# A mixture-of-experts stage in tiles of 128 rows instead of 256, with the biases prepared by GpSimd

## The chip, the cores and the metric

The kernel runs on one core of a Trainium2 chip. The metric is the device time of one execution in microseconds (us). The engines are TensorE (PE in the profile; PEld is its weight load), VectorE (DVE), ScalarE (ACT), GpSimd (POOL) and SyncE (SP, which here only issues DMAs). Each has its own sequencer, which carries out register arithmetic, waits and branches; the profile marks those with a q (PEldq is TensorE's sequencer).

## What is computed

The reference takes x (8 batches of 512 tokens, 256 wide), adds a gated cross attention, and then a gated mixture of experts, both behind a layer norm:

```python
x = x + tanh(g_xattn) * xattn(layernorm(x), ctx, Wq, Wkv, Wc)
x = x + tanh(g_ffn) * ffn(layernorm(x), gate_w, w1, b1, w2, b2)

def ffn(x, gate_w, w1, b1, w2, b2):          # 8 experts, 2 per token
    top_v, top_i = top_k(x @ gate_w, 2)
    comb = zeros(N, E).at[token, top_i].add(softmax(top_v))
    for e in range(8):
        h = gelu(x @ w1[e] + b1[e])          # 256 -> 1024
        out = out + comb[:, e] * (h @ w2[e] + b2[e])
```

In the attention each token takes the one row of the context with the highest score, and then attends with 16 heads over the rows so taken. The change lies in the mixture of experts.

## The kernel before

**Two stages.** `flow` is the first stage, up to about 520 us: attention, layer norm and gating, batch by batch, in a pipeline whose order is written out by hand in steps. Meanwhile the experts' weights are loaded, split into a bf16 high and a bf16 low part, and kept in SBUF (`w_split`). For each of its two experts, every token's normalised row is scattered by GpSimd into that expert's queue in HBM (L611). A row in a queue has 260 numbers: 256 values, the two weights of the token (already times tanh of the gate), its first expert, and its token number. At the end `tile_tables` (L144 to L172, on VectorE) works out for each tile of rows which expert it belongs to (`expert_of`) and where in `queue` it starts (`row_of`), and SyncE writes a tile of padding rows behind the end of each queue (`pad_queues`, L175). `general_select` and `general_attend` are a slow path, skipped at run time (the branch of `in_general`, L2200), which isn't taken with these inputs.

**The experts' stage** (`experts`, in the functions below) runs over `N_TILES` tiles of `TILE` rows. All rows of a tile belong to one expert; a queue's last tile is padded, and tiles left over are read from a block of padding rows. 8 x 512 tokens with 2 experts give 8192 rows, so with `TILE` 256 there are (8192 + 8 x 255)//256 = 39 tiles, 9984 rows. Each engine has a program of its own, a body per tile, and `over_tiles` (L2216) runs it: some tiles written out, the rest in a loop on the engine (L2220) with two bodies, so that buffers alternate. They meet by semaphores only:

- SyncE reads the tile's number of row into a register and loads the rows (`load`, L2243), two tiles ahead, once `x_turned` and `tail_taken` say that the buffer is free. Before the first loads it issues those of all b1 and b2 (L2239, L2240).
- TensorE's body i (L2408) is `turn(i+1)`, `layer1(i)`, `layer2(i-1)`. `turn` transposes the rows into `ps_x`. `layer1` reads the tile's expert into a register (`load_expert`, L2229) and does 48 matmuls: for each of 8 blocks f of the 1024 hidden values, 2 halves kt of the input, and three products (high weight with high and low x, low weight with high x). The weights are stationary, the tile's rows move. They go to four banks `ps_h` of two blocks each; each bank waits until the gelu of the tile before has read it. `layer2` has the hidden values stationary, 128 tokens at a time, and the weights w2, 256 columns, moving: 2 x 24 matmuls, after all of `h_lo`. In both, the weights' address depends on the register with the expert (L2390, L2404).
- ScalarE's body i: `x_hi` of tile i+1 (a cast to bf16, L2288), then eight gelu with b1 added (L2299), two for each bank.
- VectorE's body i: `prepare(i+1)` (the rows' last four columns into `tails`, the expert's b1 into `bias`, the weight of each row, and `x_lo`), then `h_lo` in four pieces (L2356: the hidden values less their bf16 high part), then `finish(i-1)`: second layer plus b2 (L2342), times the row's weight (L2345).
- GpSimd's body i (L2264): the token numbers as integers (L2269, L2271), then two indirect DMAs of 128 rows (L2273) that add y to the output in HBM. A tile's adds wait for those of the tile before.

```python
def layer2(i, s):
    e = load_expert(pe, i)
    pe.wait_ge(h_lo_ready, PAIRS * (i + 1))
```

Of the kernel before, what the change touches and what calls it, by code (L numbers as in the profile page):

```python
# [22 lines left out]
TILE = 2 * P  # L23
# [120 lines left out]
def tile_tables(v, chain, k, scratch):  # L144

    table = N_TILES * E
    mine, past = (scratch[:, c * table:(c + 1) * table].rearrange("p (i e) -> p i e", e=E) for c in range(2))
    full = scratch[:, 2 * table:2 * table + E * (QUEUE // TILE)].rearrange("p (e n) -> p e n", e=E)
    first_row = scratch[:, 2 * table + E * (QUEUE // TILE):][:, 0:N_TILES]
# [12 lines left out]
    chain.step(v.tensor_reduce(k.valid[:], mine, AX.X, ALU.add))  # L162
# [5 lines left out]
    chain.then(v.tensor_scalar(k.left[:], k.tile_row[:], -float(DUMMY), None, ALU.add))  # L168
    chain.then(v.tensor_tensor(k.valid[:], k.valid[:], k.left[:], ALU.mult))
    chain.then(v.scalar_tensor_tensor(out=k.valid[:], in0=k.valid[:], scalar=float(DUMMY), in1=first_row, op0=ALU.add,  # L170
                                      op1=ALU.add))
    chain.then(v.tensor_copy(k.row_of[:], k.valid[:]))  # L172


def pad_queues(sp, k, padded, before):  # L175

    for at in [sp.value_load(k.pad_at[0:1, n:n + 1], min_val=0, max_val=DUMMY) for n in range(E)]:
        sp.dma_start(k.queue[bass.ds(at, TILE)].rearrange("(s p) c -> p s c", p=P), k.padding[:, None, :].to_broadcast([P, 2, ROW])).then_inc(padded, 16)
    sp.wait_ge(padded, 16 * (before + E))


def program(nc, x, ctx_t, g, wq_t, wkv_t, wc_t, gate_w, w1, b1_t, w2, b2, out):
# [11 lines left out]
    with ExitStack() as whole:  # L194
# [30 lines left out]
        k.valid, k.left = sb(whole, "valid", [P, N_TILES]), sb(whole, "left", [P, N_TILES])  # L225
# [7 lines left out]
        flow(nc, k, sem, sb, ps)  # L233

        general = Programs(), Programs()
        general_select(nc, k, sem, sb, ps, general[0])
        general_attend(nc, k, sem, sb, ps, general[1])
# [3 lines left out]
def flow(nc, k, sem, sb, ps):  # L241
# [6 lines left out]
    with ExitStack() as own:  # L248
# [180 lines left out]
        def _(sp):  # L429
# [65 lines left out]
            sp.dma_start(k.queue[DUMMY:DUMMY + TILE].rearrange("(s p) c -> p s c", p=P), k.padding[:, None, :].to_broadcast([P, 2, ROW])).then_inc(k.padded, 16)  # L495
# [277 lines left out]
        def _(dve):  # L773
# [232 lines left out]
            tile_tables(v, chain, k, x_in[:].rearrange("p t d -> p (t d)"))  # L1006
# [1160 lines left out]
def experts(nc, k, sem, sb, ps, general):  # L2167
    with ExitStack() as own:
# [3 lines left out]
        xg = [sb(own, f"xg{s}", [P, 2, ROW]) for s in range(2)]  # L2172
        tails = sb(own, "tails", [P, N_TILES, 2, 4])
        weight = sb(own, "weight", [P, N_TILES, 2])
        part_a, part_b = sb(own, "part_a", [P, 2]), sb(own, "part_b", [P, 2])
        bias = [sb(own, f"bias{s}", [P, FC]) for s in range(2)]
        x_hi = [sb(own, f"x_hi{s}", [P, KT, TILE], BF16) for s in range(2)]
# [4 lines left out]
        y = [sb(own, f"y{s}", [P, 2, D]) for s in range(2)]  # L2182
        token_f, token_at = sb(own, "token_f", [P, 2]), sb(own, "token_at", [P, 2], I32)

        ps_x = ps(own, "ps_x", [P, KT, TILE])
        ps_h = [ps(own, f"ps_h{n}", [P, 2, TILE]) for n in range(FC // 2)]
        ps_y = [ps(own, f"ps_y{s}", [P, 2, D]) for s in range(2)]
# [3 lines left out]
        tail_taken, x_hi_ready, x_lo_ready = sem("tail_taken"), sem("x_hi_ready"), sem("x_lo_ready")  # L2191
        h_ready, gelu_done, h_lo_ready = sem("h_ready"), sem("gelu_done"), sem("h_lo_ready")
        y_summed, y_biased, y_weighted, added = sem("y_summed"), sem("y_biased"), sem("y_weighted"), sem("added")
        dve_steps, pool_steps = k.dve_steps, k.pool_steps
        PAIRS = FC // 2

        select_met, attend_met, pads_placed, tables_met = (sem("select_met"), sem("attend_met"), sem("pads_placed"),
                                                           sem("tables_met"))

        def in_general(engine, select_all, attend_all, finish=None):  # L2200
            flag = engine.value_load(k.wide[0:1, 0:1], min_val=0, max_val=1)  # L2201
            with engine.If(flag > 0):
                select_all(engine)
# [12 lines left out]
        def over_tiles(engine, body):  # L2216

            body(0, 0, 0, True, True)
            body(1, 0, 1, True, True)
            with engine.Fori(1, (N_TILES - 3) // 2) as j:  # L2220
                body(2 * j, j, 0, True, True)
                body(2 * j + 1, j, 1, True, True)
# [3 lines left out]
        def first(i, n=1):  # L2226
            return isinstance(i, int) and i < n

# [4 lines left out]
        def _(sp):  # L2233
# [4 lines left out]
            in_general(sp, general[0].sp, general[1].sp, pad)  # L2238
            sp.dma_start(b1_sb[:], k.b1_t).then_inc(bias_loaded, 16)  # L2239
# [3 lines left out]
            def load(i, s):  # L2243
                row = sp.value_load(k.row_of[0:1, bass.ds(i, 1)], min_val=0, max_val=DUMMY)  # L2244
                sp.dma_start(xg[s][:], k.queue[bass.ds(row, TILE)].rearrange("(s p) c -> p s c", p=P)).then_inc(row_loaded[s], 16)

            def body(i, half, s, more, two_more):
                if two_more:

                    sp.wait_ge(x_turned, i + 1)  # L2250
                    sp.wait_ge(tail_taken, i + 1)
                    load(i + 2, s)

            load(0, 0)
            load(1, 1)
# [3 lines left out]
        def _(pool):  # L2259
            in_general(pool, general[0].pool, general[1].pool)  # L2260
# [3 lines left out]
            def body(i, half, s, more, two_more):  # L2264
                if not first(i):

                    pool.wait_ge(added, 32 * i)
                pool.wait_ge(y_weighted, i + 1)
                chain.then(g.tensor_tensor(token_f[:], tails[:, bass.ds(i, 1), :, 3].rearrange("p a s -> p (a s)"),  # L2269
                                           k.ones_f[:, 0:2], ALU.mult))  # L2270
                chain.then(g.tensor_copy(token_at[:], token_f[:]))  # L2271
                for t in range(2):
                    pool.indirect_dma_start(k.out_rows, bass.IndirectOffsetOnAxis(ap=token_at[:, t:t + 1], axis=0),  # L2273
                                            y[s][:, t, :], None, bounds_check=B * L - 1, oob_is_err=False,
                                            compute_op=ALU.add).then_inc(added, 16)
                chain.restart()

            over_tiles(pool, body)
            pool.wait_ge(added, 32 * N_TILES)

        @block.scalar
        def _(act):
# [7 lines left out]
            def body(i, half, s, more, two_more):  # L2290
                if more:
                    split_x(i + 1, 1 - s)
                if not first(i, 2):
                    act.wait_ge(y_summed, i - 1)
                for n in range(PAIRS):
                    act.wait_ge(h_ready, PAIRS * i + n + 1)
                    for c in range(2):
                        f = 2 * n + c
                        last = a.activation(hidden[s][:, f, :], ps_h[n][:, c, :], ACT.Gelu, bias=bias[s][:, f:f + 1])  # L2299
# [6 lines left out]
        def _(dve):  # L2306
# [3 lines left out]
            def tables():  # L2310
                pad_places(v, chain, k, pads_placed)
                tile_tables(v, chain, k, hidden[0][:].rearrange("p f t -> p (f t)"))
# [3 lines left out]
            dve.wait_ge(bias_loaded, 32)  # L2316

            def prepare(i, half, s):


                e = load_expert(dve, i)
                dve.wait_ge(row_loaded[s], 16 * (half + 1))
                tail = tails[:, bass.ds(i, 1)].rearrange("p a s c -> p (a s) c")
                v.tensor_copy(tail, xg[s][:, :, D:ROW]).then_inc(tail_taken, 1)
                v.tensor_copy(bias[s][:], b1_sb[:, bass.ds(e, 1), :].rearrange("p a f -> p (a f)"))
                dve.wait_ge(tail_taken, i + 1)
                this = k.tile_expert[:, bass.ds(i, 1)]
                chain.step(v.scalar_tensor_tensor(out=part_a[:], in0=tail[:, :, 2], scalar=this, in1=tail[:, :, 0],
                                                  op0=ALU.is_equal, op1=ALU.mult))
                chain.then(v.scalar_tensor_tensor(out=part_b[:], in0=tail[:, :, 2], scalar=this, in1=tail[:, :, 1],  # L2330
                                                  op0=ALU.not_equal, op1=ALU.mult))
                chain.step(v.tensor_tensor(weight[:, bass.ds(i, 1), :].rearrange("p a s -> p (a s)"), part_a[:], part_b[:], ALU.add))
# [3 lines left out]
            def finish(i, s):  # L2336
                dve.wait_ge(y_summed, i + 1)
                if not first(i, 2):
                    dve.wait_ge(added, 32 * (i - 1))
                e = load_expert(dve, i)  # L2340
                b2_own = b2_all[:, bass.ds(e, 1), :].to_broadcast([P, 2, D])
                v.tensor_tensor(y[s][:], ps_y[s][:], b2_own, ALU.add).then_inc(y_biased, 1)  # L2342
                dve.wait_ge(y_biased, i + 1)
                for t in range(2):
                    last = v.tensor_scalar(y[s][:, t, :], y[s][:, t, :],  # L2345
                                           weight[:, bass.ds(i, 1), t:t + 1].rearrange("p a s -> p (a s)"), None, ALU.mult)
# [102 lines left out]
```

## Time and profile before

| | us |
|---|---|
| Median of 3 runs | 994.2 |
| Lowest and highest | 994.14, 994.46 |
| Span of the profiled execution, first to last instruction | 992.7 |
| What lies around the span, as the median less the span | 1.5 |
| PE busy | 832.3 (84%) |
| VectorE busy | 517.9 (52%) |
| GpSimd busy | 438.1 (44%) |
| ScalarE busy | 376.7 (38%) |

The profile comes from one execution. Its own time is known as its span; the runs' times are those of whole executions. Spans and windows count from its first instruction. A matmul's record lasts until its result is written, so records of one stream overlap, and the distance between starts is what a matmul costs there. Register arithmetic, loads of a register (TENSOR_LOAD) and waits don't count as busy; they appear in the view of a single line, with the engine's name and a q.

### The profile page before, as it was taken

Reading aid. Unit: us, or ns where it says so; the run is one execution under the profiler, and the core shown is the slowest. Engines: PE = TensorE matmul, PEld = TensorE weight load, DVE = VectorE, ACT = ScalarE, POOL = GpSimd, SP = SyncE. Lnnn points to the kernel's source line nnn. Section 1 sums busy time; section 2 is a strip of 40 time slices with the busy share of each in tenths; the row PEclk is TensorE's granted clock in tenths of the full one; section 3 lists DMA queues with packets and bytes.
Section 4 is the critical chain, followed back from the end, with each engine's and each line's share of the span. In section 5 each row is a group of like instructions: output and inputs, shape, how many; then the busy total and the mean of one; then the engine's idle time right before and its main releaser. Section 6 shows DMA issues by size and latency. Waiting matters only on the chain. (4 is left out here: it accounts for less than half of the span.)

```text
span 992.7 us, 20863 instructions
## 1 busy us (share of the span) xinstructions
PE 832.3 (84%) x6508; PEld 579.8 (58%) x6509; DVE 517.9 (52%) x1534; ACT 376.7 (38%) x770; POOL 438.1 (44%) x475
## 2 busy tenths in 40 slices
PE   3675899899898989887610899999999999999994
PEld 1243345344343534433310699899989989988984
DVE  3475567766766677762330345444544454454451
ACT  1312263636363544666320333333333433333330
POOL 4766463666566545436541033333433343333334
PEclk9867899989997989898755799999999999999998
DMA  4653424433445261244224122221332233223210
GB/s 160 147 108 107 75 66 90 129 82 108 97 128 98 64 136 49 82 134 138 77 74 165 56 44 46 48 45 33 56 48 41 43 58 48 43 47 49 44 14 1
DMA packets 65691, 76.40 MB, mean 77 GB/s; under 512 B 7392, under 2 KB 59360, under 8 KB 65504
## 3 DMA queue, kind: packets, MB, share of 16 engines
q1 hardware_dynamic: 51328, 58.74, 22.7%
q0 software_dynamic: 14304, 16.93, 9.6%
q8 instruction: 30, 0.49, 0.2%
q14 instruction: 29, 0.24, 0.1%
HBM read 47.68 MB, written 29.53 MB: 78 GB/s over the span
## 5 line engine op out<-in xcount | busy, mean ns | idle before, releaser
L2389 PE MATMUL ps_h<-x_hi,w_split 128*128 128x256 bf16 x1248 | 212.7, 274 | 0.0
L2403 PE MATMUL ps_y<-w_split,hidden 128*128 x1248 | 206.4, 273 | 0.0
L698 ACT ACTIVATE prob<-ps_a 128x512 f32<-128x512 f32 x192 | 113.0, 603 | 181.5 <-PE ps_a L1127 108.2
L2389 PE MATMUL ps_h<-x_lo,w_split 128*128 128x256 bf16 x624 | 171.0, 274 | 0.0
L2403 PE MATMUL ps_y<-w_split,h_lo 128*128 x624 | 170.1, 273 | 0.0
L2299 ACT ACTIVATE hidden<-ps_h,bias 128x256 f32<-128x256 f32 x312 | 131.1, 471 | 88.6 <-PE ps_h L2389 88.6
L849 DVE TENSOR_REDUCE row_max<-ps_d 128x2 f32<-128x384 f32 x237 | 127.9, 551 | 60.8 <-PE ps_d L1107 59.2
L2273 POOL DMA_INDIRECT out<-y,token_at x78 | 131.0, 1680 | 43.8 <-POOL token_at L2271 30.3
L2389 PEld LDWEIGHTS ps_h<-x_hi,w_split 128*128 x1248 | 122.8, 98 | 14.5
L2403 PEld LDWEIGHTS ps_y<-w_split,hidden 128*128 128x128 bf16 x1248 | 122.1, 98 | 14.1
L2269 POOL TENSOR_TENSOR token_f<-tails,ones_f 128x2 f32<-128x2 f32 x39 | 7.8, 200 | 267.5 <-DVE y L2345 266.3
L2342 DVE TENSOR_TENSOR y<-ps_y,b_all 128x512 f32<-128x512 f32 x39 | 27.0, 692 | 174.5 <-PE ps_y L2403 174.5
L1107 PE MATMUL ps_d<-k_st,w_split 96*128 96x192 bf16 x474 | 84.5, 268 | 25.7 <-DVE row_max L849 19.2
L2356 DVE TENSOR_TENSOR h_lo<-hidden 128x512 bf16<-128x512 f32 x156 | 99.7, 686 | 11.3 <-ACT hidden L2299 10.3
L2288 ACT CAST x_hi<-ps_x 128x512 bf16<-128x512 f32 x39 | 22.9, 586 | 213.5 <-PE ps_x L2376 213.5
L635 POOL TENSOR_TENSOR w_split<-w_stage,w_split 128x1024 bf16<-128x1024 f32 x32 | 68.0, 2132 | 63.8 <-ACT w_split L770 63.8
L1107 PEld LDWEIGHTS ps_d<-k_st,w_split 96*128 96x128 bf16 x474 | 40.0, 103 | 77.6 <-DVE row_max L849 32.0
L1144 PE MATMUL ps_o<-prob,v_st 128*32 128x512 f32 x512 | 77.1, 678 | 3.0 <-ACT prob L698 3.0
L611 POOL DMA_INDIRECT queue<-rows,slot x64 | 62.9, 982 | 19.4 <-issue 17.1
L2389 PEld LDWEIGHTS ps_h<-x_lo,w_split 128*128 x624 | 61.4, 98 | 7.4
L2403 PEld LDWEIGHTS ps_y<-w_split,h_lo 128*128 128x128 bf16 x624 | 61.1, 98 | 7.1
L1064 PE MATMUL ps_d<-ctx_sb,q_t 128*128 128x512 f32 x112 | 57.8, 640 | 2.2 <-DVE row_max L849 1.4
(206 smaller groups left out, 1070.8 us busy)
## 6 DMA issues: line engine op xcount, KB each, us to landing
w_stage<-w SPq DMA_DIRECT2D x32, 512.0 KB, 4.1
xg<-queue SPq DMA_DIRECT2D x39, 260.0 KB, 2.8
w_split<-q_split SPq DMA_DIRECT2D x24, 256.0 KB, 7.9
x_in<-x SPq DMA_DIRECT2D x8, 512.0 KB, 3.8
ctx_sb<-ctx_t SPq DMA_DIRECT2D x8, 512.0 KB, 3.6
x<-x SPq DMA_DIRECT2D x8, 512.0 KB, 3.8
q_split<-q_hl SPq DMA_DIRECT2D x16, 256.0 KB, 3.5
out<-x SPq DMA_DIRECT2D x8, 512.0 KB, 5.0
```

What stands on the lines that cost most here:

```text
L611: pool.indirect_dma_start(k.queue[:], bass.IndirectOffsetOnAxis(ap=slot[:, t, c:c + 1], axis=0), rows[:, t, :], None).then_inc(scattered, 16)
L635: g.tensor_tensor(lo, stage, hi, ALU.subtract).then_inc(w_lo, 1)
L698: a.activation(prob[n % 2][:, j, :], ps_a[i % 2][:], ACT.Exp, scale=SCALE).then_inc(exp_ready, 1)
L849: v.tensor_reduce(row_max[:, t, 2 * pair:2 * pair + 2], bank[:, 0:2 * SLOTS].rearrange("p (h r) -> p h r", h=2), AX.X, ALU.max).then_inc(m ...
L1064: last = t_.matmul(ps_da[n][:], q_t[:, kt, t * P:(t + 1) * P], ctx_sb[:, kt, :], start=(kt == 0), stop=(kt == KT - 1))
L1107: last = t_.matmul(ps_da[n][:, c * SLOTS:(c + 1) * SLOTS], q_st[m % 3][0:ROW_MAX, 2 * pair + c, t * P:(t + 1) * P], k_st[0:ROW_MAX, m % 3, ...
L1144: last = t_.matmul(ps_o[j * VW:(j + 1) * VW, :], values, probs, start=(key_tile == 0), stop=(key_tile == SLOT_TILES - 1))
L2273: pool.indirect_dma_start(k.out_rows, bass.IndirectOffsetOnAxis(ap=token_at[:, t:t + 1], axis=0), y[s][:, t, :], None, bounds_check=B * L ...
L2299: last = a.activation(hidden[s][:, f, :], ps_h[n][:, c, :], ACT.Gelu, bias=bias[s][:, f:f + 1])
L2356: v.tensor_tensor(h_lo[s][:, both, :], hidden[s][:, both, :], h_hi[s][:, both, :], ALU.subtract).then_inc(h_lo_ready, 1)
L2389: last = t_.matmul(ps_h[n][:, c, :], k.w1_split[:, bass.ds(e, 1), part, kt, f].rearrange("p a f -> p (a f)"), xs[s][:, kt, :], start=(q == ...
L2403: last = t_.matmul(ps_y[s][:, t, :], hs[s][:, f, token], k.w2_split[:, bass.ds(e, 1), part, f, :].rearrange("p a d -> p (a d)"), start=(q ...
```

## The change

`TILE` becomes 128, so that there are (8192 + 8 x 127)//128 = 71 tiles, 9088 rows. With it:

- The first layer's matmuls have 128 moving columns in place of 256; the second layer has one group of 24 per tile in place of two; `turn` has two transposes in place of four. Banks of PSUM stay whole: `ps_h` and `ps_y` are half used.
- `tails` and `weight` become rings of four small tiles (`RING`), no longer one table over all tiles; the loop over tiles has four bodies.
- GpSimd makes the biases: it copies the expert's b1 into `bias`, and forms `bias2`, the tile's b2 times each row's weight (a ring of four as well), one tile ahead. ScalarE waits for the first (`bias1_ready`), VectorE for the second (`bias2_ready`). GpSimd's body i scatters tile i-1 and then prepares tile i+1.
- VectorE's `finish` is one pass: y = second layer x weight + bias2. It no longer loads the expert's number. `h_lo` is formed in two pieces, of four blocks each.
- SyncE issues the first two row loads ahead of those of b1 and b2.
- `tile_tables` works with tables of 71 x 8 entries, for which it needs two scratch tiles. The slow path takes over semaphores of `flow`, cleared by GpSimd in its branch.

```diff
-TILE = 2 * P
+TILE = P
...
-        sp.dma_start(k.queue[bass.ds(at, TILE)].rearrange("(s p) c -> p s c", p=P), k.padding[:, None, :].to_broadcast([P, 2, ROW])).then_inc(padded, 16)
+        sp.dma_start(k.queue[bass.ds(at, TILE)], k.padding[:]).then_inc(padded, 16)
...
-            for i in range(2 * ((N_TILES - 3) // 2), N_TILES):
-                body(i, i // 2, i % 2, i + 1 < N_TILES, i + 2 < N_TILES)
...
+            for i in range(RING):
+                body(i, i // 2, i % RING)
+            with engine.Fori(1, (N_TILES - 3) // RING) as j:
+                for r in range(RING):
+                    body(RING * j + r, 2 * j + r // 2, r)
+            for i in range(RING * ((N_TILES - 3) // RING), N_TILES):
+                body(i, i // 2, i % RING)
...
+            load(0, 0)
+            load(1, 1)
             sp.dma_start(b1_sb[:], k.b1_t).then_inc(bias_loaded, 16)
...
+            def prepare(i, r):
+                e = load_expert(pool, i)
+                if not known(i, 2):
+                    pool.wait_ge(gelu_done, PAIRS * (i - 1))
+                g.tensor_copy(bias[r % 2][:], b1_sb[:, bass.ds(e, 1), :].rearrange("p a f -> p (a f)")).then_inc(bias1_ready, 1)
+                pool.wait_ge(weight_ready, i + 1)
+                g.tensor_tensor(bias2[r][:], b2_all[:, bass.ds(e, 1), :].rearrange("p a d -> p (a d)"),
+                                weight[r][:].to_broadcast([P, D]), ALU.mult).then_inc(bias2_ready, 1)
+
+            def scatter(i, r):
+                if not known(i, 1):
+                    pool.wait_ge(added, 16 * i)
                 pool.wait_ge(y_weighted, i + 1)
...
+            def body(i, half, r):
+                if not known(i, 1):
+                    scatter(i - 1, (r - 1) % RING)
                 chain.restart()
+                if within(i, N_TILES - 1):
+                    prepare(i + 1, (r + 1) % RING)
...
+                act.wait_ge(bias1_ready, i + 1)
...
+                    dve.wait_ge(added, 16 * (i - RING + 1))
...
+                dve.wait_ge(bias2_ready, i + 1)
+                if not known(i, 2):
+                    dve.wait_ge(added, 16 * (i - 1))
+                v.scalar_tensor_tensor(out=y[s][:], in0=ps_y[s][:, 0:D], scalar=weight[r][:], in1=bias2[r][:],
+                                       op0=ALU.mult, op1=ALU.add).then_inc(y_weighted, 1)
...
-                for n in range(PAIRS):
-                    dve.wait_ge(gelu_done, PAIRS * i + n + 1)
...
+                for n in range(HALVES):
+                    dve.wait_ge(gelu_done, PAIRS * i + PAIRS // HALVES * (n + 1))
...
-                for t in range(2):
-                    token = slice(t * P, (t + 1) * P)
-                    for q, (f, hs, part) in enumerate(terms):
...
+                for q, (f, hs, part) in enumerate(terms):
+                    last = t_.matmul(ps_y[s][:, 0:D], hs[s][:, f, :],
+                                     k.w2_split[:, bass.ds(e, 1), part, f, :].rearrange("p a d -> p (a d)"),
+                                     start=(q == 0), stop=(q == len(terms) - 1))
```

## Rows read from the trace of the kernel before

**Rows 1.** The page's head: span, and PE and its granted clock in 40 slices.

```profile
span 992.7 us, 20863 instructions
...
PE   3675899899898989887610899999999999999994
...
PEclk9867899989997989898755799999999999999998
```

**Rows 2.** Table by stretches: us, then busy (x instructions) of PE, PEld, DVE, ACT, POOL; PEclk, DMA, GB/s.

```profile
400.00:500.00 100.00, 74.81 (x473) 35.15 (x469) 47.93 (x195) 55.23 (x100) 50.52 (x45) 0.86 0.34 109
600.00:700.00 100.00, 100.00 (x918) 90.04 (x917) 46.86 (x118) 35.52 (x81) 33.99 (x37) 1.00 0.26 44
```

**Rows 3.** The chain in order of time, 700 to 725 us: start us, us, what.

```profile
702.28 5.24 PE ps_h L2389 x48
...
713.20 5.24 PE ps_h L2389 x48
```

**Rows 4.** Lines L2373, L2230, L2389, L2403, 700 to 710.5: ns min/median/max, first and last start.

```profile
L2373 PEldq FUSED_REGOPS  x1: 42/42/42, 700.2 to 700.2; - x1
...
L2230 PEldq TENSOR_LOAD <-expert_of x2: 301/302/303, 700.4 to 705.6; - x2
...
L2389 PEldq FUSED_REGOPS  x32: 46/46/51, 701.2 to 705.4; - x32
...
L2403 PEldq FUSED_REGOPS  x16: 46/46/60, 706.4 to 708.3; - x16
```

**Rows 5.** Line L2389 at the stage's start, 552.4 to 554.6 us.

```profile
L2389 PEldq FUSED_REGOPS  x17: 46/46/51, 552.5 to 554.5; - x17
...
L2389 PE MATMUL ps_h<-x_hi,w_split x7: 421/421/421, 552.5 to 554.4; 128*128 128x256 bf16 x7
```

**Rows 6.** TensorE's timeline in the first stage: start us, us from first start to last end.

```profile
385.93 0.50 PE L1107 MATMUL ps_d<-k_st,w_split 96*128 96x192 bf16 x4
386.27 0.54 PE L1074 MATMUL ps_r<-ones_bf,chosen 128*128 128x1 bf16 x16
...
386.92 0.26 PE L1107 MATMUL ps_d<-k_st,w_split 96*128 96x192 bf16 x1
...
438.51 0.40 PE L1117 MATMUL ps_r<-ident_bf,max_split 128*32 128x128 bf16 x4
```

**Rows 7.** Line L1117, 438.4 to 439 us.

```profile
L1117 PE MATMUL ps_r<-ident_bf,max_split x4: 219/219/229, 438.5 to 438.7; 128*32 128x128 bf16 x4
```

**Rows 8.** Line L2220, the loop over tiles, on TensorE's sequencer, whole run.

```profile
L2220 PEldq COMPARE_BRANCH  x17: 83/215/242, 590.7 to 940.0; - x17
```

**Rows 9.** VectorE's timeline, 713 to 720 us.

```profile
713.73 0.69 DVE L2342 TENSOR_TENSOR y<-ps_y,b_all 128x512 f32<-128x512 f32 x1 [4.42 <-PE ps_y L2403]
```

**Rows 10.** GpSimd's timeline, 704 to 708 us.

```profile
704.43 0.18 POOL L2269 TENSOR_TENSOR token_f<-tails,ones_f 128x2 f32<-128x2 f32 x1 [6.15 <-DVE y L2345]
...
705.68 1.56 POOL L2273 DMA_INDIRECT out<-y,token_at  x1 [0.82 <-POOL token_at L2271]
707.55 1.99 POOL L2273 DMA_INDIRECT out<-y,token_at  x1 [0.30 <-issue]
```

**Rows 11.** ScalarE's timeline, 707 to 709 us.

```profile
706.62 0.47 ACT L2299 ACTIVATE hidden<-ps_h,bias 128x256 f32<-128x256 f32 x1
707.56 0.84 ACT L2299 ACTIVATE hidden<-ps_h,bias 128x256 f32<-128x256 f32 x2 [0.47 <-PE ps_h L2389]
```

**Rows 12.** A costly group of the page on GpSimd.

```profile
L635 POOL TENSOR_TENSOR w_split<-w_stage,w_split 128x1024 bf16<-128x1024 f32 x32 | 68.0, 2132 | 63.8 <-ACT w_split L770 63.8
```

**Rows 13.** SyncE's DMA issues, 515 to 545 us.

```profile
522.10 6.30 SPq L178 DMA_DIRECT2D queue<-padding  x8
541.38 0.35 SPq L2239 DMA_DIRECT2D b_sb<-b_t  x1
```

**Rows 14.** The chain in order of time, 548 to 566 us.

```profile
542.98 5.98 DMA xg<-queue
...
552.71 7.22 PE ps_h L2389 x48
```

More of the change, by code:

```diff
@@ L2170, in experts @@
         b2_all = sb(own, "b2_all", [P, E, D])
[L2172 to L2175, printed above, removed]
+        RING = 4
+        xg = [sb(own, f"xg{s}", [P, ROW]) for s in range(2)]
+        tails = [sb(own, f"tails{r}", [P, 4]) for r in range(RING)]
+        weight = [sb(own, f"weight{r}", [P, 1]) for r in range(RING)]
+        part_a, part_b = sb(own, "part_a", [P, 1]), sb(own, "part_b", [P, 1])
         bias = [sb(own, f"bias{s}", [P, FC]) for s in range(2)]
+        bias2 = [sb(own, f"bias2{r}", [P, D]) for r in range(RING)]
         x_hi = [sb(own, f"x_hi{s}", [P, KT, TILE], BF16) for s in range(2)]
@@ L2216, in over_tiles, with known, within @@
         def over_tiles(engine, body):
[L2218 to L2222, printed above, removed]
-            for i in range(2 * ((N_TILES - 3) // 2), N_TILES):
-                body(i, i // 2, i % 2, i + 1 < N_TILES, i + 2 < N_TILES)
-        def first(i, n=1):
+            for i in range(RING):
[5 more added lines that the diff above has]
+                body(i, i // 2, i % RING)
+        def known(i, n):
             return isinstance(i, int) and i < n
+        def within(i, n):
+            return not isinstance(i, int) or i < n
         def load_expert(engine, i):
@@ L2288, in split_x, with body @@
                 a.copy(x_hi[s][:], ps_x[:]).then_inc(x_hi_ready, 1)
-            def body(i, half, s, more, two_more):
-                if more:
+            def body(i, half, r):
+                s = r % 2
+                if within(i, N_TILES - 1):
                     split_x(i + 1, 1 - s)
-                if not first(i, 2):
+                act.wait_ge(bias1_ready, i + 1)
+                if not known(i, 2):
                     act.wait_ge(y_summed, i - 1)
@@ L2298, in body @@
                         f = 2 * n + c
-                        last = a.activation(hidden[s][:, f, :], ps_h[n][:, c, :], ACT.Gelu, bias=bias[s][:, f:f + 1])
+                        last = a.activation(hidden[s][:, f, :], ps_h[n][:, c * TILE:(c + 1) * TILE], ACT.Gelu, bias=bias[s][:, f:f + 1])
                     last.then_inc(gelu_done, 1)
@@ L2337, in finish @@
                 dve.wait_ge(y_summed, i + 1)
[L2338 to L2346, printed above, removed]
@@ L2347, in finish @@
-                last.then_inc(y_weighted, 1)
-            def body(i, half, s, more, two_more):
-                chain.restart()
-                if more:
-                    prepare(i + 1, half + s, 1 - s)
-                for n in range(PAIRS):
-                    dve.wait_ge(gelu_done, PAIRS * i + n + 1)
-                    both = slice(2 * n, 2 * n + 2)
-                    v.tensor_tensor(h_lo[s][:, both, :], hidden[s][:, both, :], h_hi[s][:, both, :], ALU.subtract
+                dve.wait_ge(bias2_ready, i + 1)
@@ new lines, in finish, with body @@
+                if not known(i, 2):
+                    dve.wait_ge(added, 16 * (i - 1))
+                v.scalar_tensor_tensor(out=y[s][:], in0=ps_y[s][:, 0:D], scalar=weight[r][:], in1=bias2[r][:],
+                                       op0=ALU.mult, op1=ALU.add).then_inc(y_weighted, 1)
+            def body(i, half, r):
+                s = r % 2
+                chain.restart()
+                if within(i, N_TILES - 1):
+                    prepare(i + 1, half + s, (r + 1) % RING)
+                for n in range(HALVES):
+                    dve.wait_ge(gelu_done, PAIRS * i + PAIRS // HALVES * (n + 1))
+                    part = slice(n * FC // HALVES, (n + 1) * FC // HALVES)
+                    v.tensor_tensor(h_lo[s][:, part, :], hidden[s][:, part, :], h_hi[s][:, part, :], ALU.subtract
@@ L2371, in turn @@
                 pe.wait_ge(row_loaded[s], 16 * (half + 1))
-                if not first(i):
+                if not known(i, 1):
                     pe.wait_ge(x_lo_ready, i)
                 for kt in range(KT):
-                    for t in range(2):
-                        last = t_.transpose(ps_x[:, kt, t * P:(t + 1) * P], xg[s][:, t, kt * P:(kt + 1) * P], k.ident[:])
+                    last = t_.transpose(ps_x[:, kt, :], xg[s][:, kt * P:(kt + 1) * P], k.ident[:])
                 last.then_inc(x_turned, 1)
@@ L2382, in layer1 @@
                 for n in range(PAIRS):
-                    if not first(i):
+                    if not known(i, 1):
                         pe.wait_ge(gelu_done, PAIRS * (i - 1) + n + 1)
```

146 lines of the change are left out of this document (78 added, 68 removed).

## The prediction

> **What bounds the kernel now.** I read the page's head first [rows 1]: from slice 24 on PE is busy nine tenths or more at a full granted clock, so the experts' stage, from about 552 us to the end, is TensorE's. The table by stretches agrees [rows 2]: in 600 to 700 us PE is busy for all 100 us at clock 1.00, VectorE for 47, GpSimd for 34. The chain in order of time gives the pattern of one tile [rows 3]: 48 matmuls of the first layer in 5.24 us, and the next tile's begin at 713.20, 10.92 us after 702.28; between lie as many of the second layer and four transposes, 0.44 us if a matmul of either layer costs the same. 39 tiles make 425.9 us. A matmul of 256 columns takes 5.24/48 = 0.109 us.
>
> The view of single lines shows a second worker, which this busy PE hides [rows 4]. PEldq is TensorE's sequencer. The weights are picked by the tile's expert, known only at run time, so ahead of the matmuls it computes their addresses (FUSED_REGOPS): 32 for the first layer (kt, part and f give 2x2x8), 16 for the second. In the tile shown it works at the first layer's from 701.2 to 705.4, while the matmuls run from 702.28 on [rows 3], and at the second's from 706.4 to 708.3. The steps are (705.4-701.2)/31 = 0.135 us, the instructions for the waits among them, and (708.3-706.4)/15 = 0.127. That this is the sequencer's own pace, not a full queue that pushes back, is to be seen at the stage's start [rows 5]: there matmuls go at half clock (a record lasts 0.42 us), and the seven with the high x, of ten in all, from 552.5 to 554.4, 0.21 us each, yet 17 address instructions go from 552.5 to 554.5, again 0.125 each. Two loads of the expert's number, at 700.4 and 705.6, delay what follows: 1.0 us passes from the wait at 700.2 to the first address at 701.2, and 1.0 from 705.4 to 706.4 [rows 4]. So from 700.2 to 708.3, plus one step, the sequencer has 8.2 us of work for one tile, hidden now below 10.92.
>
> **The change, part by part.**
>
> *Tiles of 128 rows.* Per tile, the second layer's 48 matmuls of 256 columns become 24, and 4 transposes become 2. The first layer keeps 48, of 128 columns. Their pace has near rows [rows 6, 7]: four bf16 matmuls of 128 columns take 0.40 us with 0.22 for the last, so (0.40-0.22)/3 = 0.06; four of 192 columns (0.50-0.26)/3 = 0.08; sixteen of one column, each with a full 128x128 weight load, 0.54, under 0.034 each. The weight load hides, then, and columns set the pace: I take 0.056, near the row of 128 columns, between 0.055 (half of 0.109) and 0.08. PE itself needs 48 x 0.056 + 24 x 0.109 + 0.22 = 5.5 us per tile, at most 6.7.
>
> But the sequencer's work per tile stays: the same 32 and 16 addresses, two expert loads, the same waits. What goes is the second half of the rows, whose matmuls use addresses again: 16 instructions serve 48 matmuls [rows 4]. 8.2 us, with 0.1 for the instructions of the turn that stand before 700.2, and 0.2 of branch [rows 8] in every fourth tile, make 8.35. That exceeds 5.5, so it becomes the pace: 71 x 8.35 = 592.9 us against 425.9, **+167.0**. Bounds: 8.0, if a part of the pauses was the queue's; 8.6, if branch and waits cost more. That is 568.0 to 610.6.
>
> *Bias times weight ahead on GpSimd, scatter one tile late.* The first layer's bias copy goes from VectorE to GpSimd, behind the scatter, and ScalarE now waits for it. Queued behind that wait are eight gelu and the next x_hi; for the gelu wait h_lo, and PE, which uses ps_h again. The path from the end of a second layer: VectorE's product and sum, 0.5 us (between 0.35 and the 0.69 of 512 columns [rows 9]); GpSimd's start, 0.2; index conversion, pause and descriptors, 704.43 to 707.24, 2.8 [rows 10]; the bias copy, 0.2, like the small pass there; ScalarE's start, 0.1 to 0.4. That is 4.0 us. Then eight gelu: two of 256 columns take 0.84 with 0.47 for one, 0.37 apart [rows 11]; for 128 I take 0.27, between 0.19 (half) and 0.37, so 2.2 us (1.5 to 3.0); and 0.7 for the last h_lo, still a pass of 512 columns [rows 9]. At 8.35 us a tile PE ends layer2(i-1) some 0.8 us into body i+1 (issued from 6.2 us on, 2.6 long); the bias for i+1 is there at 4.8, its first pair of gelu done at 5.4, the last at 7.0, h_lo at 7.7. PE needs the first pair at 8.35 + 1.0 and h_lo at 8.35 + 6.2: 4 us of slack, which is the cover, so I cost this at nothing. The product b2 x weight, of 256 columns on GpSimd, lies between the 0.18 of two columns [rows 10] and the 2.1 of 1024 [rows 12]; it stands behind the bias copy, and even 2.1 is done before the next scatter. The new waits for places in the rings of four, for gelu of tile i-1 and for the weight look back to work that is over by then.
>
> *h_lo in two pieces, weight and bias in one pass.* VectorE loses two of four waits, the bias copy, one pass over y and both expert loads; at 47 of 100 us [rows 2] it was off the path and stays there.
>
> *Queues.* SP issues 71 row loads in place of 39, each half as large. Its padding writes halve too, and the tables on VectorE grow from 312 to 568 columns; both end around 522 to 528 us, and SP's next DMA is at 541.4 [rows 13]: nothing. On SP the first two row loads pass ahead of b1 and b2. The first landed 5.98 us after 542.98 [rows 14]; it is now issued at 541.4, so 1.6 us at least, and 5 if it no longer shares with b2: 3. The biases land as late as now, but the first gelu waits for them, not PE. At half clock the first layer of tile 0 took 7.22 us [rows 14] in place of 5.24; after, half clock costs the first tile under 1 us: -1. At the end one scatter goes, 1.9 us (707.55 less 705.68 [rows 10]), and an expert load, about 1: -3.
>
> *Sum.* 992.7 + 167.0 - 3 - 1 - 3 = 1152.7 us of span. The runs' median of 994.2 lies 1.5 us above the profiled execution's span, so **1154.2 us**. With the bounds of the tile it is 1129 to 1172, with those of start and end 1126 to 1174.
>
> **Rivals.**
>
> *A. GpSimd's chain sets the pace.* If the sequencer were no limit, the next one is a loop of one tile: gelu(i) waits for its bias, which stands behind scatter(i-2), which waits for y(i-2), which VectorE forms after h_lo(i-1), which follows gelu(i-1). By the terms above 2.2 + 0.7 + 4.0 = 6.9 us: 71 x 6.9 = 489.9, so 992.7 + 64.0 - 7 + 1.5 = 1051 us. The order is in the code; against it speak [rows 4, 5]. It decides where the sequencer needs less than 6.9 us.
>
> *B. The clock falls.* PE would execute 5.5 of 8.35 us. Where it was busy for 75% of a stretch the mean clock was 0.86 [rows 2]. At half clock a tile costs PE twice 5.35 = 10.7 us; were three tiles in ten so, 0.3 x 2.35 x 71 = 50 more, 1204 us; with all of them 1321. Against it: the pauses here are short and spread over the tile.
>
> *C. Faster.* If neither sequencer nor GpSimd holds PE back, 71 x 5.5 = 390.5, so 992.7 - 35.4 - 7 + 1.5 = 952 us: 9088 rows in place of 9984. It needs address work that costs far less than the rows show; the turning point is (425.9+7)/71 = 6.1 us per tile. [Rows 5] speak against it. The Trainium skill (TensorE: Matmul & The Clock Gate, Back-to-back issue gap) has a rule against this rival: a sustained stream of weight loads and 128-column matmuls takes about 81 ns for each. An estimate by that page: 48 x 0.081 + 2.84 = 6.7 us a tile and 1039 us, slower even without the sequencer. The trace disagrees: 0.06 for such a matmul, and 0.08 only at 192 columns [rows 6, 7].
>
> **How the numbers follow.** Chances: the forecast 0.80, B 0.09, A 0.06, C 0.05. The forecast's own range, with a margin for steps that no row shows, is 1110 to 1200. Up to 1235 it takes in B's milder half; A, C, B's far end and the forecast's own tails are the two in ten left out. About 0.2%, 2 us, is what a measurement can tell here: faster by more is C, 0.05; within it almost nothing, 0.01; slower 0.94.
>
> **What would show it.** Right: one tile takes 8.2 to 8.5 us; PE pauses inside the first layer, whose 48 matmuls spread over some 4.4 us, and the pauses aren't put down to ScalarE; 48 address instructions per tile follow each other without a long gap; the granted clock stays near 1.00; ScalarE's first gelu waits for GpSimd, yet PE doesn't wait for gelu. Wrong: PE waits for gelu or h_lo and a tile takes 6.9 us (A); tiles of over 10 us at clock 0.5 (B); 5.5 us without pauses (C). The weakest number is the 0.125 us per address: at 0.10 a tile would take 1.2 us less, and the time be 1069.

## The result and the profile after

The changed kernel takes 1148.7 us (median of 4 runs, 1147.5 to 1149.6) against 994.2 (four runs by then, 992.1 to 994.5): a ratio of 1.157, with a 95% interval of 1.155 to 1.159. The prediction was 1154.2, slower.

The head of the page after, to be held against [rows 1]: from slice 20 on PE is busy for eight or nine tenths and no longer for all of each slice, at a full granted clock.

```profile
span 1147.8 us, 26798 instructions
...
PE   4576898989898988630988888888888888888886
...
PEclk9787998989898989665999999999999999999999
```

The table by stretches (columns as in [rows 2]): PE has pauses now, and no other engine comes near being full.

```profile
600.00:700.00 100.00, 88.69 (x883) 69.64 (x883) 33.19 (x95) 30.27 (x108) 33.44 (x60) 1.00 0.19 31
```

The chain in order of time (start us, us, what), which answers to [rows 3]. The starts 700.65 and 734.19 are four tiles apart, so one takes 33.54/4 = 8.385 us. The first layer's 48 matmuls of 128 columns take 4.4 us in place of 5.24 of 256, and ahead of the second layer there is "issue", time in which PE waits for nothing that the profile shows.

```profile
700.65 4.43 PE ps_h L2430 x48
705.08 0.76 issue
705.84 2.83 PE ps_y L2442 x24
...
717.76 4.40 PE ps_h L2430 x48
...
734.19 4.43 PE ps_h L2430 x48
```

What fills that "issue" shows in the view of single lines, TensorE's sequencer, the tile at 700 us; it answers to [rows 4]. 32 addresses go from 700.5 to 704.8, (704.8-700.5)/31 = 0.139 us apart with the instructions for waits, as long as the matmuls take; then the expert's number is loaded (704.9), and 16 addresses follow from 705.7 on, (707.6-705.7)/15 = 0.127. The queue of work has no gap: the sequencer is the busy one. The loop's four bodies are more code than two, but nothing points to its fetching: over the whole run the profile's two instruction queues moved 0.52 and 0.25 MB, 0.49 and 0.24 before, and the second layer's addresses are 0.127 apart in both kernels.

```profile
L2430 PEldq FUSED_REGOPS  x32: 46/46/51, 700.5 to 704.8; - x32
...
L2256 PEldq TENSOR_LOAD <-expert_of x2: 298/299/300, 699.8 to 704.9; - x2
...
L2442 PEldq FUSED_REGOPS  x16: 46/46/60, 705.7 to 707.6; - x16
```

The waits from 600 to 1100 us (engine, line, what it waited for: us, times, longest): ScalarE does wait for GpSimd's bias, 3.3 us at most, but where PE waits it is almost always "issue".

```profile
ACT hidden L2345 <- POOL bias L2296: 188.6, 58, 3.3
...
PEld ps_y L2442 <- issue: 54.3, 59, 1.0
...
PEld ps_h L2430 <- issue: 22.6, 60, 0.8
PE ps_y L2442 <- DVE h_lo L2398: 12.6, 15, 0.8
```

The last row is a trap. In one tile of four the chain steps from PE back to VectorE's h_lo, and from there through gelu and bias to the scatter, as though GpSimd's loop set the pace:

```profile
713.73 0.70 DVE h_lo L2398
714.44 0.20 issue
714.64 2.85 PE ps_y L2442 x24
```

The order in the code rules that out: the second layer at 714.64 belongs to the tile before and uses that tile's h_lo. This h_lo is the first half of the next tile's, and its second half starts only after the matmuls that are said to wait for it, as VectorE's timeline shows:

```profile
713.73 0.69 DVE L2398 TENSOR_TENSOR h_lo<-hidden 128x512 bf16<-128x512 f32 x1 [3.06 <-ACT hidden L2345]
714.76 0.69 DVE L2398 TENSOR_TENSOR h_lo<-hidden 128x512 bf16<-128x512 f32 x1 [0.34 <-ACT hidden L2345]
```

Both count on one semaphore, and its latest increment happened to fall just before. The third experiment checks this on the chip.

### The profile page after: what moved, and what is told of

Its sections match the earlier page's. It is cut to its first block, busy times and chain, and to the rows that moved or that the text cites. A ratio compares the mean times of both kernels' runs of the same rounds, so it can differ in the third digit from the quotient of the medians.

```text
span 1147.8 us, 26798 instructions
## 1 busy us (share of the span) xinstructions
PE 932.8 (81%) x7862; PEld 612.0 (53%) x7863; DVE 519.7 (45%) x1594; ACT 404.1 (35%) x1058; POOL 490.8 (43%) x675
## 4 chain that ended last, share of the span: by engine, by line
PE 40%; issue 6%; POOL 3%; DVE 2%; ACT 1%; POOLq 1%; DMA 1%; ACTq 0%; SPq 0%
PE ps_h L2430 21%; PE ps_y L2442 17%; PE ps_x L2417 1%; POOL token_at L2307 1%; POOL bias L2296 1%; ACT hidden L2345 1%; DVE h_lo L2398 1%; DVE y L2387 1%; POOLq L2256 0%; POOL out L2308 0%; POOL token_f L2306 0%; DMA xg<-queue 0%; DMA out<-y,token_at 0%; POOLq L2243 0%; ACTq L2342 0%
## 5 line engine op out<-in xcount | busy, mean ns | idle before, releaser
L2430 PE MATMUL ps_h<-x_hi,w_split 128*128 128x128 bf16 x2272 | 313.2, 228 | 10.5 <-issue 8.3
L2430 PEld LDWEIGHTS ps_h<-x_hi,w_split 128*128 x2272 | 217.6, 96 | 92.1 <-issue 27.3
L2430 PE MATMUL ps_h<-x_lo,w_split 128*128 128x128 bf16 x1136 | 249.8, 220 | 0.0
L2345 ACT ACTIVATE hidden<-ps_h,bias 128x128 f32<-128x128 f32 x568 | 155.1, 383 | 229.6 <-POOL bias L2296 213.6
L2308 POOL DMA_INDIRECT out<-y,token_at x71 | 114.2, 1608 | 57.2 <-POOL token_at L2307 57.2
L2430 PEld LDWEIGHTS ps_h<-x_lo,w_split 128*128 x1136 | 112.5, 99 | 0.0
L1117 PE MATMUL ps_d<-k_st,w_split 96*128 96x192 bf16 x474 | 84.5, 268 | 25.6 <-DVE row_max L859 19.1
L2332 ACT CAST x_hi<-ps_x 128x256 bf16<-128x256 f32 x71 | 26.5, 373 | 208.0 <-PE ps_x L2417 208.0
L2387 DVE SCALAR_TENSOR_TENSOR y<-ps_y,weight,bias 128x256 f32<-128x256 f32 x71 | 34.3, 484 | 116.5 <-PE ps_y L2442 116.5
L2298 POOL TENSOR_TENSOR bias<-b_all,weight 128x256 f32<-128x256 f32 x71 | 84.7, 1192 | 0.0
L1117 PEld LDWEIGHTS ps_d<-k_st,w_split 96*128 96x128 bf16 x474 | 40.0, 103 | 77.4 <-DVE row_max L859 31.9
L2296 POOL COPY bias<-b_sb 128x8 f32 x71 | 55.3, 778 | 20.3 <-DMA b_all<-b 20.1
```

The costliest lines, as they stand in the source:

```text
L1117: last = t_.matmul(ps_da[n][:, c * SLOTS:(c + 1) * SLOTS], q_st[m % 3][0:ROW_MAX, 2 * pair + c, t * P:(t + 1) * P], k_st[0:ROW_MAX, m % 3, ...
L2296: g.tensor_copy(bias[r % 2][:], b1_sb[:, bass.ds(e, 1), :].rearrange("p a f -> p (a f)")).then_inc(bias1_ready, 1)
L2298: g.tensor_tensor(bias2[r][:], b2_all[:, bass.ds(e, 1), :].rearrange("p a d -> p (a d)"), weight[r][:].to_broadcast([P, D]), ALU.mult).the ...
L2345: last = a.activation(hidden[s][:, f, :], ps_h[n][:, c * TILE:(c + 1) * TILE], ACT.Gelu, bias=bias[s][:, f:f + 1])
L2430: last = t_.matmul(ps_h[n][:, c * TILE:(c + 1) * TILE], k.w1_split[:, bass.ds(e, 1), part, kt, f].rearrange("p a f -> p (a f)"), xs[s][:, ...
```

## The experiments

The theory is the prediction's: the addresses set the pace. Its rivals are a pace set by the matmuls of 128 columns and their weight loads, and rival A, GpSimd's loop.

**1. No addresses on TensorE.**

```diff
-                                             k.w1_split[:, bass.ds(e, 1), part, kt, f].rearrange("p a f -> p (a f)"),
+                                             k.w1_split[:, 0, part, kt, f],
...
-                                     k.w2_split[:, bass.ds(e, 1), part, f, :].rearrange("p a d -> p (a d)"),
+                                     k.w2_split[:, 0, part, f, :],
```

> The changed kernel, with TensorE's weights always those of expert 0: no load of the expert's number and no address on TensorE's sequencer; the choice of the expert by TensorE is left out of the computation, all else stays. Theory (the sequencer's address work sets the pace, 8.385 us per tile): the pace falls to the next limit, GpSimd's loop: from the rows of the changed kernel 3.19 (y to the end of the bias copy) + 0.19 + 2.18 (eight gelu) + 1.1 (last h_lo and y) = 6.7 us per tile, so 1148.7 - 71 x 1.69 = 1029 us, between 1010 and 1060; ScalarE then waits for the bias, and PE for gelu. Rival 1 (the pace is that of 128-column matmuls with their weight loads): nothing changes, 1145 to 1152. Rival 2 (GpSimd's loop was the pace before already, at 8.4): nothing changes either. If GpSimd's loop is shorter than I think, up to 5.5 us per tile, 944.

Measured: 1028.5 us. The rival of matmuls and weight loads falls, and so does the second: GpSimd's loop is shorter than 8.385. But it is the next bound, as rival A had it. In the waits from 650 to 800 us ScalarE's waits for the bias have grown, to 97.1/23 = 4.2 us each from 188.6/58 = 3.3, PE now waits for gelu, and "issue" is gone:

```profile
ACT hidden L2345 <- POOL bias L2296: 97.1, 23, 4.3
...
PEld ps_h L2429 <- ACT hidden L2345: 27.6, 23, 1.3
```

**2. No addresses, and the bias ahead of the scatter.** The run above with, in GpSimd's body:

```diff
+                if within(i, N_TILES - 1):
+                    prepare(i + 1, (r + 1) % RING)
                 if not known(i, 1):
                     scatter(i - 1, (r - 1) % RING)
                 chain.restart()
-                if within(i, N_TILES - 1):
-                    prepare(i + 1, (r + 1) % RING)
```

> As the run with expert 0's weights always (TensorE's choice of the expert left out), and GpSimd's preparation of the next tile's biases stands ahead of the scatter in its body. Theory: with both the sequencer's addresses and the wait for the scatter gone, PE's own work is the pace, 5.5 us per tile: 1148.7 - 71 x 2.885 = 944 us; up to 975 if the scatter's own chain of one tile (y, indices, descriptors, landing; 5.3 to 5.9 us) binds. The difference to the run without the reordering is the price of GpSimd's place, 1.2 us per tile or 85 us. Rival (the reordering is worth nothing even then): the same time as that run, within 5 us.

Measured: 947.6 us. GpSimd's place was the bound of the first run, at (1028.5-947.6)/71 = 1.14 us per tile. Here PE works without a pause, and the chain of waits holds nothing else; a tile takes 706.88-701.36 = 5.52 us, the 5.5 of rival C:

```profile
701.36 2.68 PE ps_h L2429 x48
704.04 2.62 PE ps_y L2440 x24
...
706.88 2.68 PE ps_h L2429 x48
```

**3. The bias ahead of the scatter, addresses kept.** The same edit on the changed kernel alone.

> The changed kernel with GpSimd's preparation of the biases ahead of its scatter, and nothing else. Theory (sequencer): ScalarE gets its bias some 3 us sooner and waits for the matmuls instead; the time stays at 1145 to 1152. Rival A (GpSimd's chain takes part in the pace): faster by more than 20 us.

Measured: 1150.2 us (1148.8 to 1151.1), no gain. ScalarE waits for PE and no longer for GpSimd, and PE still for "issue" (waits, 600 to 700 us). So GpSimd took no part in the pace, and the chain's step into its loop was a wrong attribution.

```profile
ACT hidden L2345 <- PE ps_h L2430: 27.3, 47, 1.3
...
PEld ps_y L2442 <- issue: 11.4, 12, 1.0
```

**4. The kernel before without addresses.** The edit of run 1 on tiles of 256 rows.

> The kernel before (tiles of 256 rows) with expert 0's weights always: TensorE's choice of the expert, its loads and addresses are left out. Theory: with 256 columns the matmuls take 10.92 us per tile and hide 8.2 us of address work; 992 to 996 us, at most 2 less from the start and the end of the stage. Rival (addresses cost TensorE time whatever the size of a tile): 39 x up to 2.5 us less, some 900 to 970.

Measured: a ratio of 1.0009 (0.9997 to 1.0021). In tiles of 256 rows the address work costs nothing that can be measured.

**5. A dose in between.** The changed kernel with the edits of runs 1 and 2, but fixed weights in the second layer alone.

> A dose between the changed kernel and the one with expert 0's weights throughout: only the second layer always uses expert 0's weights (that choice is left out), the first layer still picks its own; GpSimd prepares ahead of its scatter. Theory: the 16 addresses and one load of the expert's number, 2.04 + 0.74 = 2.8 us, leave the sequencer's 8.385 us; at least 5.6 us per tile remain, at most 7.3 if the sequencer can't run ahead over the whole second layer: 950 to 1072, and I take the middle, 6.2 us per tile, 994. If addresses cost TensorE nothing: as the reordered kernel with both, 1150.

Measured: 1011.8 us, inside the bounds and 18 above the middle; a tile takes 708.23-701.94 = 6.29 us:

```profile
701.94 3.30 PE ps_h L2430 x48
705.24 2.78 PE ps_y L2441 x24
...
708.23 3.28 PE ps_h L2430 x48
```

The first layer is still stretched, from 2.68 to 3.3. Its load of the expert (0.67 by run 6) and its block of addresses (4.43 in the changed kernel's chain) would take 5.1; 1.8 of that lay behind second-layer matmuls already queued, some 17 of 0.109. That is how far the sequencer got ahead of PE in this run: an estimate, from these rows. The trace agrees: TensorE's load of the expert's number (line L2256) starts at 706.2, and the second layer ends at 705.24 + 2.78 = 708.02.

**6. One register load more.**

```diff
             def layer1(i, s):
+                load_expert(pe, i)
                 e = load_expert(pe, i)
```

> The changed kernel with the tile's expert number loaded a second time ahead of the first layer (no other work). Theory: this load stands in line on TensorE's sequencer, 0.74 us per tile, so 71 x 0.74 = 53 more than 1148.7: 1201, between 1190 and 1210. Rivals that put the pace elsewhere (matmuls, GpSimd): hidden, 1145 to 1152.

Measured: 1196.1 us, 47.4 more, 0.67 per tile, not 0.74. The trace has the same number: the two loads start 0.7 us apart.

```profile
L2256 PEldq TENSOR_LOAD <-expert_of x2: 298/299/300, 703.0 to 703.7; - x2
```

A single register load, whose value nothing uses, costs the kernel its full time. That makes the sequencer the pace, by adding as well as by taking away.

**7. Addresses taken off TensorE, with the right weights.** VectorE copies the expert's first-layer weights to a place that is known beforehand; GpSimd's order as in run 2.

```diff
+            def copy_w1(i, s):
+                e = load_expert(dve, i)
+                if not known(i, 2):
+                    dve.wait_ge(h_ready, PAIRS * (i - 1))
+                v.tensor_copy(w1_now[s][:].rearrange("p n t f -> p (n t f)"),
+                              k.w1_split[:, bass.ds(e, 1)].rearrange("p a n t f -> p (a n t f)")).then_inc(w1_copied, 1)
...
                     prepare(i + 1, half + s, (r + 1) % RING)
+                    copy_w1(i + 1, 1 - s)
...
+                pe.wait_ge(w1_copied, i + 1)
...
-                                             k.w1_split[:, bass.ds(e, 1), part, kt, f].rearrange("p a f -> p (a f)"),
+                                             w1_now[s][:, part, kt, f],
```

> Computes the whole reference. The changed kernel, GpSimd preparing first, and VectorE copying the tile's expert's first-layer weights (4096 bf16 numbers in each partition) into one of two fixed buffers a tile ahead: the first layer's 32 addresses and one load of the expert go from TensorE's sequencer; 2.8 us for the second layer stay. Theory: the pace becomes PE's own work, 5.5 us per tile, if VectorE, busy 2.8 us per tile, has room for the copy, which is so at up to some 2 us: 945 to 960, faster than the kernel before. If the copy takes 4.3 us (one number in each cycle's time, by the 0.69 us of 512 columns some 5.5 at most), VectorE's 7.1 to 8.3 us per tile set the pace, 1058 to 1145. If addresses were not the pace: 1150 or more.

Measured: 959.2 us, a ratio of 0.967 (0.965 to 0.969): faster than both kernels. The page's kind of group, for 600 to 700 us, prices the copy at 1.25 us (busy, mean ns), and VectorE, 76% busy there, has room for it:

```profile
L2387 DVE COPY w_now<-w_split 128x4096 bf16 x18 | 22.6, 1254 | 6.9 <-PE ps_h L2441 4.5 <-issue 2.4
```

The chain there is PE alone, with the second layer at 2.73 where run 2 has 2.62:

```profile
705.87 2.68 PE ps_h L2441 x48
708.55 2.73 PE ps_y L2453 x24
```

**8. The start: row loads first, in the kernel before.** `load(0, 0)` and `load(1, 1)` moved ahead of the loads of b1 and b2.

> The kernel before with the first two row loads issued ahead of those of b1 and b2, as in the change. My term for the start was 3 us, between 1.6 and 5, so a ratio of 0.997 (0.995 to 0.9984). If the first load's time were hidden: 1.000.

Measured: 1.0005 (0.9993 to 1.0017), nothing. The first transposes start at 546.06, where the row load of [rows 14] landed only at 548.96; but the second group, which waits for x_lo, starts at 554.66, and with it the first layer, 3 us later than in [rows 5] (TensorE's timeline):

```profile
546.06 1.11 PE L2376 MATMUL ps_x<-ident,xg 128*128 128x128 f32 x4 [31.97 <-DMA xg<-queue]
554.66 1.09 PE L2376 MATMUL ps_x<-ident,xg 128*128 128x128 f32 x4 [7.48 <-DVE x_lo L2334]
```

VectorE forms x_lo behind its bias copy, and that waited for b2 (its timeline):

```profile
553.15 0.17 DVE L2324 COPY tails<-xg 128x8 f32<-128x8 f32 x1 [30.02 <-DMA b_all<-b]
```

This execution is the slowest of the twelve, 997.97 us beside a median of 993.5, so its 3 us are more than the median lost. That the others lose at x_lo about what they gain at the transposes is argued, not shown.

**9. The start: b1 and b2 first, in the changed kernel.** The same two pairs of lines, the other way round.

> The changed kernel with the loads of b1 and b2 again ahead of the first two row loads. By the traces of both kernels the first row load then starts about 1 us later and lands 6.0 instead of 3.3 us after its start: 3 to 4.3 us slower than the changed kernel of the same group of runs, some 1152. Rival (the start's gain has other causes, such as the padding): no difference.

Measured: 1153.0 us (ratio to before 1.1609, 1.1583 to 1.1635) beside 1149.2 for the changed kernel in run 11: 3.8 more, as expected, though the intervals overlap. The chain bears it out: the row load starts 1.6 us after the first of the biases' (539.21) and takes 5.53 instead of 3.31.

```profile
539.21 0.35 SPq L2277
...
540.80 5.53 DMA xg<-queue
```

**10. The kernel of run 7, with the second layer's register load moved.** `load_expert(pe, i - 1)` goes ahead of `layer1(i)`.

> Computes the whole reference. The kernel with VectorE's copy of the first layer's weights; TensorE now loads the expert's number for layer2(i-1) ahead of layer1(i), while it still has matmuls of the second layer queued. Its second layer took 2.73 to 2.75 us there and 2.62 without any address, with the load standing between the layers. Theory: the 0.11 us of each tile go, 71 x 0.11 = 8 us, so 951 and a ratio of 0.958 to before. Rival (the 0.11 are the addresses' own): 959, 0.967.

Measured: 952.8 us, 0.960 (0.957 to 0.962), the fastest kernel that computes the reference. The second layer is back at 2.62, a tile at 712.70-707.18 = 5.52:

```profile
707.18 2.68 PE ps_h L2441 x48
709.86 2.62 PE ps_y L2452 x24
...
712.70 2.68 PE ps_h L2441 x48
```

**11. The changed kernel, in the same group.**

> The changed kernel itself, as the measure for the two runs on its start: 1148 to 1150.

Measured: 1149.2 us, 1.1589 (1.1563 to 1.1614).

**12. The start: row loads first, bias copy behind x_lo, in the kernel before.** The loads as in run 8, and on ScalarE and VectorE:

```diff
+                if first(i):
+                    act.wait_ge(bias_loaded, 33)
...
-            dve.wait_ge(bias_loaded, 32)
...
                 v.tensor_tensor(x_lo[s][:], ps_x[:], x_hi[s][:], ALU.subtract).then_inc(x_lo_ready, 1)
+                if first(i):
+                    dve.wait_ge(bias_loaded, 32)
+                    v.tensor_copy(bias[s][:], b1_sb[:, bass.ds(e, 1), :].rearrange("p a f -> p (a f)")).then_inc(bias_loaded, 1)
```

> The kernel before with the first two row loads ahead of b1 and b2, and VectorE copying the first tile's bias behind x_lo instead of ahead of it (ScalarE's first gelu waits for that copy). In the run with the loads moved alone the first transposes came 2.9 us earlier, but x_lo stood behind the bias copy, which waited for b2 until 552.5, and the first matmuls came 3.0 us later. Theory: without that the first layer starts some 2.8 us earlier than in the kernel before, ratio 0.9972, 991.3 against 994.2. Rival (gelu now waits for the biases and gives it back): 1.000.

Measured: 0.997 (0.9957 to 0.9984), as expected. In its trace the first layer starts 547.67-540.82 = 6.85 us after SyncE's first load, where before it was 552.50-541.38 = 11.1. So the loads' order, which bought nothing alone (run 8), pays once nothing behind them waits for the biases; the bias copy's move alone was not run.

## Why the prediction was right, and where its terms were off

**The pace of a tile: right.** The sum was 8.2 + 0.1 + 0.05 = 8.35 us; the trace has 8.385, so the stage grew by 71 x 8.385 - 425.9 = 169.4 us, not 167.0. The weakest number, 0.125 us per address, held: 0.127 in the second layer, 0.139 in the first with the instructions for waits among them. Runs 1 and 2 (taking it away), 5 (a part of it), 6 (adding to it) and 4 (no effect in tiles of 256 rows) show the cause.

**PE's own 5.5 us: right,** and visible only with the sequencer out of the way: 5.52 in runs 2 and 10. The page named in rival C (the Trainium skill, TensorE: Matmul & The Clock Gate, Back-to-back issue gap) would have given 6.7 us there; its 81 ns for a weight load with a matmul stand against 2.68/48 = 56 ns measured. Rival C's 952 us is close to what the kernels with PE as the pace took: 947.6 in run 2, 952.8 in run 10.

**The cover over GpSimd's chain: right, by terms that were not.** From the end of y to the end of the bias copy I put 0.2 + 2.8 + 0.2 = 3.2 us and the trace of after has 3.19 (709.19 to 712.38 in its chain), by terms that cancel: from the first index pass to the copy it is 711.57-709.33 = 2.24, since the copy starts while the scatter's record still runs, and the copy takes 0.8, not 0.2. Before the first scatter the same copy does take 0.19 (547.17), so the 0.2 was right for GpSimd alone and wrong beside a scatter. `bias2` takes 1.2, inside 0.18 to 2.1. The slack was as forecast: the eight gelu from 712.56 on take 2.18 us, so the first pair is done by some 713.2, and PE uses that bank again at 717.76, 4.6 us later, where I had 4. GpSimd's timeline after, the stage's first copy and one tile:

```profile
547.17 0.19 POOL L2296 COPY bias<-b_sb 128x8 f32 x1 [20.13 <-DMA b_all<-b]
...
709.33 0.19 POOL L2306 TENSOR_TENSOR token_f<-tails,ones_f 128x1 f32<-128x1 f32 x1 [4.65 <-DVE y L2387]
...
710.55 1.61 POOL L2308 DMA_INDIRECT out<-y,token_at  x1 [0.78 <-POOL token_at L2307]
711.57 0.80 POOL L2296 COPY bias<-b_sb 128x8 f32 x1
711.73 1.22 POOL L2298 TENSOR_TENSOR bias<-b_all,weight 128x256 f32<-128x256 f32 x1
```

Rival A's loop came to 6.9; in run 1, where it sets the pace, the same view has the copies 710.91-704.16 = 6.75 apart:

```profile
704.16 0.81 POOL L2296 COPY bias<-b_sb 128x8 f32 x1
...
710.91 0.78 POOL L2296 COPY bias<-b_sb 128x8 f32 x1
```

**The clock: right.** The granted clock is 1.00 in the stretch from 600 to 700 us although PE has pauses in every tile; rival B didn't come. Its price was a little low: twice PE's 5.5 is 11.0 us a tile, not 10.7, so 1211 and 1342 us in place of 1204 and 1321.

**The start: too small.** I gave it -3. The first matmul of the first layer comes at 544.92, 7.6 us before the 552.50 of the kernel before:

```profile
539.06 3.31 DMA xg<-queue
...
544.92 4.69 PE ps_h L2430 x48
```

3.8 of that are the order of the loads, inside my 1.6 to 5: from SyncE's first load to the first layer it is 548.88-539.21 = 9.67 us in run 9 and 544.92-539.06 = 5.86 here. Some 1.5 are the smaller tile 0, which I left out: with the same order of loads it takes 11.1 us from SyncE's first load to the first layer before (541.38 to 552.50) and 548.88-539.21 = 9.7 in run 9, 0.45 of it the load's landing (5.98, 5.53) and 1.0 the turn. The other 2.3 are SyncE's earlier readiness: the eight padding writes, costed at nothing, start 1.35 sooner in this execution (520.75), take 4.0 us instead of the 6.3 of [rows 13], and the first load follows their start 18.3 us later instead of 19.3. The 1.35 are within chance: over the traces of all runs the writes start between 518.7 and 522.6, with either size. The last 1.0 comes with the size: 17.3 to 18.8 us in every trace with the smaller writes, 19.2 to 20.5 in every one with the larger. That the writes themselves cause it is argued, not shown.

**Half clock and end: too small too.** Tile 0's first layer lost 7.22-5.24 = 1.98 us to the low clock before and 4.69-4.43 = 0.26 now (its matmuls go 0.107 us apart until 548.6 and 0.056 behind), -1.7 where I had -1. From the end of the last-but-one tile's second layer, where the chain leaves PE for good, to the end of the span it is 1147.8-1135.23 = 12.6 us, 5.8 less than before (992.7-974.34 = 18.4) where I had -3. Two parts of it I mis-sized. The scatters of two tiles lie there, the second waiting for the first to land, and each loses its second DMA, issued 1.86 us after the first (977.81 to 979.67, and 983.66 to 985.53): 3.7, where I counted one scatter, 1.9. The chain of before shows both:

```profile
977.81 0.35 POOL out L2273
...
979.67 2.71 DMA out<-y,token_at
...
983.66 0.35 POOL out L2273
...
985.53 1.56 POOL out L2273
```

And VectorE's finish takes 0.5 us (1135.26 to 1135.75) instead of 2.1 (974.34 to 976.44). 0.7 of the difference is the expert load that I had at about 1; the rest I had called off the path. At the end it is on it, as the chain of after shows:

```profile
1132.41 2.82 PE ps_y L2442 x24
...
1135.26 0.49 DVE y L2387
```

The other 0.5 lies behind the issue of the last DMA, from which it is 7.2 us to the end of the span before (985.53 to 992.7) and 6.6 after (1141.18 to 1147.8); its cause stays open.

Together: 169.4 - 7.6 - 1.7 - 5.8 = 154.3, against 155.1 of span. The three terms were 8.1 us too small and the tile's 2.4 too small the other way, so part of the error cancelled: 5.7 by these sums, 160.0-155.1 = 4.9 by the span. The difference of 0.8 lies in the stage and stays open.

## What to carry to other kernels

Where an operand's place depends on a register, count the sequencer's address instructions and register loads per tile (here 0.13 and 0.67 us each) beside the matmuls' time: smaller tiles shrink the one and not the other. Copying the chosen operand to a fixed place on an engine with room can buy back more than the whole loss (run 7, with GpSimd's order changed as well), and a register load cost nothing where matmuls of 256 columns were still queued ahead of it, 0.11 us behind those of 128 (runs 10 and 7). Before believing a chain that runs through a counting semaphore, check in the code whether that increment is the one waited for.

## What the runs showed of the hardware

- TensorE's sequencer stayed the bound in a stage in which the head of the page shows PE eight to nine tenths busy: 88.7 of 100 us, of which the matmuls need 5.52/8.385 = 66%. Overlapping records, each 0.22 us long at starts 0.06 to 0.21 apart, hide the pauses.
- VectorE copied 4096 bf16 per partition in 1.25 us (run 7), while a copy of 8 f32 per partition on GpSimd took 0.8 when it started inside a scatter's record and 0.19 with no scatter running. `bias2` likewise: 1.22 and, at 547.33, 0.61.
